# A perceiver layer on one core: keys and values as pairs of 64-row matmuls, and the heads' ends moved to ScalarE and GpSimd

## What is computed

```python
x = x + xattn(layernorm(x), ctx, ctx)      # 16 heads of 64, keys and values from ctx [8192, 512]
x = x + mamba_block(layernorm(x))          # selective scan, then a gated MLP
x = x + experts(layernorm(x))              # 16 experts, top 2, and a shared one

def xattn(Q, K, V):
    q = (Q @ Wq + bq) / sqrt(64)
    k, v = K @ Wk + bk, V @ Wv + bv        # [8192, 1024] each
    a = softmax(q @ k.T)                   # per head
    return (a @ v) @ Wo + bo
```

## Time and profile before

| | us |
|---|---|
| median of 3 runs | 2430.55 (2430.43 to 2432.51) |
| profiled execution | 2432.78 |
| its span | 2431.1 |
| PE busy | 2290.2 (94%) |
| DVE busy | 1974.1 (81%) |
| ACT busy | 1616.7 (67%) |
| POOL busy | 669.3 (28%) |
| key and value stage | about 41 to 864 |
| attention | about 864 to 1738 |

### The profile page before, as it was taken

The page is one execution under the profiler, slowest core; times in us unless marked ns, Lnnn a source line. Parts: engine busy times, 40 slices in busy tenths (PEclk is TensorE's granted clock), DMA queues, the critical chain, the costliest instruction groups (busy, mean ns, idle before and its releaser), DMA issues. The chain is left out here.

```text
span 2431.1 us, 45462 instructions
## 1 busy us (share of the span) xinstructions
PE 2290.2 (94%) x17215; PEld 1187.6 (49%) x17215; DVE 1974.1 (81%) x1972; ACT 1616.7 (67%) x1974; POOL 669.3 (28%) x464
## 2 busy tenths in 40 slices
PE   7999999999999978999999999999877788989998
PEld 3333333333333346666666666666432234444554
DVE  5777777777777788999999999999679992367996
ACT  5555565555655367989999889998474442237994
POOL 1455555555555430000000000000049970020001
PEclk9999999999999989999999999999989999999999
DMA  7244555445553397333333333331240014249994
GB/s 259 88 157 156 181 166 173 156 156 179 166 174 104 114 231 201 104 100 102 107 103 101 108 101 102 102 107 61 107 174 0 0 51 157 105 155 346 407 406 166
DMA packets 168861, 360.50 MB, mean 148 GB/s; under 512 B 13337, under 2 KB 84121, under 8 KB 165081
## 3 DMA queue, kind: packets, MB, share of 16 engines
q1 hardware_dynamic: 167266, 355.27, 45.4%
q0 software_dynamic: 1280, 4.20, 0.5%
q10 hardware_dynamic: 248, 0.15, 0.0%
HBM read 252.54 MB, written 107.04 MB: 148 GB/s over the span
## 5 line engine op out<-in xcount | busy, mean ns | idle before, releaser
L473 DVE TENSOR_REDUCE kv_mx<-kv_s 128x1024 f32 (+1 forms) x512 | 595.5, 1218 | 222.6 <-PE kv_s L509 222.6
L767 DVE TENSOR_TENSOR at_pl<-at_pf,at_ph 128x1024 f16<-128x1024 f32 x512 | 621.8, 1224 | 28.1 <-ACT at_ph L716 14.1
L722 ACT ACTIVATE at_pf<-at_st 128x1024 f32<-128x1024 f32 x512 | 521.7, 1020 | 91.2 <-PE at_st L869 90.3
L842 PE MATMUL at_acc<-at_vs,at_ph 128*128 128x130 f16 x4096 | 427.5, 220 | 17.0 <-DVE at_av L773 13.9
L844 PE MATMUL at_acc<-at_vs,at_pl 128*128 128x65 f16 x4096 | 413.1, 192 | 0.0
L842 PEld LDWEIGHTS at_acc<-at_vs,at_ph 128*128 128x128 f16 x4096 | 367.4, 97 | 86.2 <-DVE at_av L773 19.8
L868 PE MATMUL at_st<-keep_big,at_k_cur 128*128 (+1 forms) x1024 | 389.4, 380 | 13.9 <-DMA keep_big<-q_dram 7.6
L844 PEld LDWEIGHTS at_acc<-at_vs,at_pl 128*128 128x128 f16 x4096 | 362.2, 98 | 57.8 <-issue 0.3
L869 PE MATMUL at_st<-keep_big,at_k_one 128*128 (+1 forms) x1024 | 389.6, 380 | 0.0
L716 ACT ACTIVATE at_ph<-at_pf 128x1024 f16<-128x1024 f32 x256 | 268.4, 1048 | 0.0
L1083 POOL MEMSET mamba_zero<- 128x2 f32 x1 | 0.1, 99 | 855.0 <-POOLq L60 855.0
(11 more groups left out here) (348 smaller groups left out, 3595.9 us busy)
## 6 DMA issues: line engine op xcount, KB each, us to landing
keep_big<-gate_up SPq DMA_DIRECT2D x17, 2048.0 KB, 13.4
at_vs<-vd SPq DMA_DIRECT2D x64, 520.0 KB, 3.6
at_k_cur<-kd SPq DMA_DIRECT2D x126, 256.0 KB, 3.8
vd<-kv_vs SPq DMA_DIRECT2D x15, 2080.0 KB, 8.2
kv_tf<-wpack SPq DMA_DIRECT2D x21, 1024.0 KB, 6.3
keep_big<-down SPq DMA_DIRECT2D x17, 1024.0 KB, 13.6
first_cf<-ctxT SPq DMA_DIRECT2D x16, 1024.0 KB, 12.5
ex_yg<-gate_up SPq DMA_DIRECT2D x8, 2048.0 KB, 13.7
```

The costliest lines, as they stand in the source:

```text
L473: nc.vector.reduce_max(mx[:, bass.ds(g * (NH * TT) + 2 * (m - TT), 2)], s1[:, m % 3, :, :], AX.X).then_inc(s1_max, 1)
L722: nc.scalar.activation(pf[:, s % FULL, :, :], st[:, s % HP % NST, :, :], ACT.Exp, scale=SCORE).then_inc(pf_ready, 1)
L767: nc.vector.tensor_tensor(pl[:, s % RING, :, :], pf[:, s % FULL, :, :], ph[:, s % RING, :, :], ALU.subtract).then_inc(pl_ready, 1)
L842: nc.tensor.matmul(own_acc[t], ph[:, s % RING, e, tok], vs[:, 2 * s + e, :], start=first, stop=False, skip_group_check=True)
```

## The change

In the key and value stage each 128-row matmul of a unit becomes two 64-row matmuls, a top on rows 0 to 63 and a bottom on rows 64 to 127, which accumulate in the same bank one after the other: the top of matmul `k` of a unit is queued next to the bottom of matmul `k - 3` (`DELAY`) of the unit before, which is in another bank, so `kp` and `vp` get two banks each and `s1` keeps two buffers instead of three. A unit's bottoms begin once its tops are done (`top_done`). Score tiles are no longer in bursts: two of them stand in each unit, after matmuls 1 and 7, seven tiles behind the count of two per unit (`BEHIND`); seven are left after chunk 15. Two more passes of `units` finish the last bottoms.

In the attention, at a head's end ACT makes the two copies of `acc`, behind its exponential of step `HP + 3` (`COPY_AT`), POOL adds and multiplies, and DVE takes only the reciprocal, behind step `HP + 5`. At the last head ACT copies after its last step, DVE does the rest.

```diff
-        kp, vp = m.ps("kp", [P, CK]), m.ps("vp", [P, CK])
-        s1 = m.ps("s1", [P, 3, 2, CK])
+        kp, vp = m.ps("kp", [P, 2, CK]), m.ps("vp", [P, 2, CK])
+        s1 = m.ps("s1", [P, 2, 2, CK])
...
+        SCORES = PAIRS * TT
+        BEHIND = 7
+        SLOTS_OF_SCORES = (1, 7)
+        UNITS = 2 * PAIRS
+        DELAY = 3
...
+            def scores(g, par, n):
...
+                pe.wait_ge(kh_ready, PAIRS * g + n // TT + 1)
+                pe.wait_ge(s1_max, g * SCORES + n + 1)
+                for e in range(2):
+                    rows = slice(e * DH, (e + 1) * DH)
+                    nc.tensor.matmul(s1[:, n % 2, e, :], keep.qh[rows, j, t * P:(t + 1) * P],
+                                     keys[rows, j, :], start=True, stop=True,
+                                     tile_position=(rows.start, 0)).then_inc(s1_ready, 1)
...
+            def top(unit, k):
+
+                bank, pairs, _ = unit
+                a, b = pairs[k]
+                first = nc.tensor.matmul(bank, a[0:DH, :], b[0:DH, :], start=(k == 0), stop=False,
+                                         skip_group_check=True, tile_position=(0, 0))
+                if k == 11:
+                    first.then_inc(top_done, 1)
+
+            def bottom(unit, k, tops):
+
+
+                bank, pairs, done = unit
+                a, b = pairs[k]
+                if k == 0:
+                    pe.wait_ge(top_done, tops)
+                last = nc.tensor.matmul(bank, a[DH:P, :], b[DH:P, :], start=False, stop=(k == 11),
+                                        skip_group_check=True, tile_position=(DH, 0))
+                if k == 11:
+                    last.then_inc(done, 1)
+
+            def units(g, par, b, now, before, before2):
+
+
+                for k in range(12):
+                    if now:
+                        top(now, k)
+                    if k < DELAY and before2:
+                        bottom(before2, 12 + k - DELAY, None)
+                    elif k >= DELAY and before:
+                        bottom(before, k - DELAY, UNITS * g + b)
+                    if k in SLOTS_OF_SCORES:
+                        scores(g, par, 2 * b + SLOTS_OF_SCORES.index(k) - BEHIND)
...
+            units(NCK, 0, 0, None, unit(1, UNITS - 1), unit(1, UNITS - 2))
+            units(NCK, 0, 1, None, None, unit(1, UNITS - 1))
+            for n in range(4 - BEHIND, 0):
+                scores(NCK, 0, n)
...
+            with pool.Fori(0, NH - 1) as h:
+                pool.wait_ge(acc_read, h * 2 + 4)
+                nc.gpsimd.tensor_tensor(osum[:, :, :], av[:, :, 0:DH], av[:, :, ONE + 2:VW], ALU.add).then_inc(sum_ready, 1)
+                pool.wait_ge(sum_ready, h + 1)
+                pool.wait_ge(rc_ready, h + 1)
+                nc.gpsimd.tensor_tensor(o[:, :, bass.ds(h * DH, DH)], osum[:, :, :],
+                                        rc[:, :].unsqueeze(2).to_broadcast([P, TT, DH]), ALU.mult).then_inc(o_ready, 1)
...
-        END_AT, CUT = 1, 20
+        END_AT, COPY_AT, CUT = 5, 3, 20
...
+            def copied(h):
+                act.wait_ge(pv_done, h * HP + HP + RING)
+                act.wait_ge(o_ready, h + 1)
+                for b in range(2):
+                    nc.scalar.activation(av[:, 2 * b:2 * b + 2, :],
+                                         acc[:, b, 0:2 * VW].rearrange("p (t c) -> p t c", c=VW),
+                                         ACT.Copy).then_inc(acc_read, 1)
...
+                if s == HP + COPY_AT:
+                    copied(h)
...
             turns(act, pair, CUT)
+            copied(NH - 1)
...
             def end(h):
-                dve.wait_ge(pv_done, h * HP + HP + RING)
-                for b in range(2):
-                    nc.vector.tensor_copy(av[:, 2 * b:2 * b + 2, :], acc[:, b, 0:2 * VW].rearrange("p (t c) -> p t c", c=VW)
-                                          ).then_inc(acc_read, 1)
                 dve.wait_ge(acc_read, h * 2 + 4)
+                nc.vector.reciprocal(rc[:, :], av[:, :, ONE]).then_inc(rc_ready, 1)
...
-                pe.wait_ge(o_ready, 2 * j + 2)
+                pe.wait_ge(o_ready, 2 * j + 3)
```

More of the change, by code:

```diff
@@ L445, in _ @@
             act.wait_ge(mt_ready, 1)
-            nc.scalar.activation(mrow[:, :], kp[0:NH * TT, 0:P], ACT.Copy).then_inc(mrow_ready, 1)
+            nc.scalar.activation(mrow[:, :], kp[0:NH * TT, 0, 0:P], ACT.Copy).then_inc(mrow_ready, 1)
             act.wait_ge(mrow_ready, 1)
@@ L498, in _ @@
         def _(pe):
[L499 to L511, removed]
@@ L513, in scores_free @@
-            def scores_free(g, tiles):
-                if isinstance(g, int) and g == 0 and tiles[-1] < TT:
-                    return
-                pe.wait_ge(kh_ready, PAIRS * g + tiles[-1] // TT)
-                pe.wait_ge(s1_max, g * (PAIRS * TT) + tiles[0] - TT + 2)
-            def chunk(g, par, uses, i, tiles):
[L521 to L530, removed]
+            def scores(g, par, n):
+                if isinstance(g, int) and g == 0 and n < 0:
+                    return
+                j, t = n // TT % PAIRS, n % TT
+                keys = ksh[par if n >= 0 else 1 - par]
+                pe.wait_ge(kh_ready, PAIRS * g + n // TT + 1)
[5 more added lines that the diff above has]
+                                     tile_position=(rows.start, 0)).then_inc(s1_ready, 1)
@@ new lines, in key_unit, with value_unit @@
+            def key_unit(par, n):
+                cols = slice(n * P, (n + 1) * P)
+                return kp[:, n % 2, :], [p for c in range(DC) for p in three(
+                    keep.wkh[:, c, cols], keep.wkl[:, c, cols], ch[par][:, c, :], cl[par][:, c, :])], k_ready
+            def value_unit(par, n):
+                tok, cols = slice(n // 2 * P, (n // 2 + 1) * P), slice(n % 2 * 512, (n % 2 + 1) * 512)
+                return vp[:, n % 2, :], [p for c in range(DC) for p in three(
+                    ch[par][:, c, tok], cl[par][:, c, tok], keep.wvh[:, c, cols], keep.wvl[:, c, cols])], v_ready
@@ L532, in chunk, with unit @@
+            def unit(par, b):
+                return value_unit(par, b // 2) if b % 2 else key_unit(par, b // 2)
+            def chunk(g, par, uses, i, tiles):
                 pe.wait_ge(ch_ready, g + 1)
                 pe.wait_ge(cl_ready, g + 1)
[L534 to L543, removed]
+                for b in range(UNITS):
+                    if b % 2:
+                        pe.wait_ge(vf_ready, VT * g + b // 2 + 1)
+                    else:
+                        pe.wait_ge(kf_ready, PAIRS * g + b // 2 + 1)
+                    prior = [unit(par, b - n) if b >= n else None if isinstance(g, int) and g == 0
+                             else unit(1 - par, UNITS + b - n) for n in (1, 2)]
+                    units(g, par, b, unit(par, b), *prior)
@@ L789, in _ @@
             low(1)
-            end(NH - 1)
+            last_end()
             for j in range(2, PAIRS - 1):
```

55 lines of the change are left out of this document (25 added, 30 removed).

## The result

The changed kernel took 2396.73 us (median of four runs, 2396.10 to 2400.49) beside 2431.20 for the kernel before on the same chip: a ratio of 0.986, 95% interval 0.9845 to 0.9875, or 34.5 us faster. Forecast were 47.2. Its profiled execution has a span of 2394.7 us, 36.4 less than before. First the page: PE's busy time, and the queues' lines.

What follows compares the result with a forecast made beforehand. PE's queue was taken to bound both stages, with DVE and ACT close behind in the attention. Gains of 34.3 + 15.3 - 2.4 = 47.2 us gave 2383.5 us for the median, range 2377 to 2408.

Steps and rivals of the forecast that it cites:

- rival (b): Key and value stage: PE's longer loop body no longer stays loaded, 8 to 25 us, say 12, giving 2396; chance 0.12.
- What bounds it: Both stages: PE's queue leads; in the attention DVE (49.93) and ACT (45.95 of 51.00 us) stand right behind.
- Part 1, burst costs: Key and value stage: each score burst's 0.213 us beyond its work goes, 16 chunks x 11, 37.5 us.
- The pair at 0.2158, not 0.227: Key and value stage: a pair of halves takes 0.2158 us; 0.227 throughout would cost 40 us.
- (c): Key and value stage: accumulating pairs don't keep 0.2158 us; at 0.25 they cost 122 us, giving 2505; chance 0.10.
- (d): Key and value stage: pairs partly overlap or `kh_ready` is late, gaining half of 34, 2400; chance 0.08.
- Weight loads hidden, waits free: Key and value stage: doubled weight loads hide behind running matmuls, and PE's added waits cost nothing.
- The loop stays loaded: Key and value stage: PE's larger loop body of two chunks is not fetched again at its returns, no cost.
- The stage's end, +3.2: End of the key and value stage: last bottoms run with nothing beside them, net 3.2 us longer.
- Heads' ends: Attention: with ACT copying, an end loses 0.22 us instead of 1.24, 15 x 1.02 = 15.3 us gained.
- Rival (a): Attention: ACT or DVE falls behind after the copy, nothing gained at heads' ends, 2399; chance 0.12.
- The last head: Attention's end: ACT's copies come before its first `oh`, delaying PE's projection by 2.4 us, bounds 1.5 to 4.

Runs made afterwards that it cites:

- unrolled: The changed kernel with PE's loop over chunks written out, 16 chunks one after the other, other engines keeping their loops: 2388.96 us, ratio 0.9814.
- switch_each: The changed kernel's schedule of single score pairs, but with whole 128-row products in place of tops and bottoms: 2494.89 us.
- fill18: The changed kernel with 18 idle matmuls of 512 columns where PE waits for the first context: 2404.11 us, ratio 0.9884.
- best: The changed kernel with PE's chunk loop written out, 18 idle matmuls before the stage, and the last head's two copies back on DVE: 2379.52 us, ratio 0.9779.
- seven_moved: The changed kernel with one of three products left out of value units and 90 idle matmuls of 32 columns ahead of PE's loop: 2317.26 us.
- before_body4: The kernel before with PE's loop body doubled to four chunks, 2140 instructions and two returns: 2445.35 us beside 2435.73.

## Why the prediction was right, and where it was off

The sign and the stated range held. The median lies 13 us above the predicted time and outside the forecast's own bounds (2378 to 2391): it falls in the wider range because rival (b), given 0.12, came true, and the missing gain is where (b) had put it, at 2396. The account that the forecast itself rested on was right in every other part that it names.

- **What bounds it.** Right: both stages follow PE's queue.
- **Part 1, burst costs.** Right, 37.5 us. In `unrolled` the stage from first matmul to transpose is 786.7 us against 819.1 before, 32.5 less; the forecast was 34.3, and the slow start takes 1.7 of it. `switch_each` shows the 0.213.
- **The pair at 0.2158, not 0.227.** Right, for all 3584. Rivals (c) and (d) are refuted: chunk intervals of 48.35, and between 100 and 742 us no row of a wait for `kh_ready`, `s1_max` or `top_done`. The 0.227 is a first step after a change only.
- **Weight loads hidden, waits free.** Right.
- **The loop stays loaded.** This is the step that failed, and it had been given 0.12. Rival (b) named the mechanism, seven or eight packets against a limit that no row showed, and 12 us; measured 10.3 over six returns. I had counted seven, one too many: seven turns have six returns. What argued against it, "a body of five is not fetched again", was true and no evidence on eight. The Trainium skill (Advanced Engine Details and Errata, ISA Cache) gives 128 KB on TensorE in lines of 16 KB. By that size alone a body touching eight lines stays, and the traces disagree: it is fetched again, nine packets a return, seven stay.
- **The start of the stage.** Not foreseen: 1.7 us more at the 1.2 GHz level. The stage's first halves find PE's clock down after its wait. `fill18` and `best` hold it at 1.00 there.
- **The stage's end, +3.2.** Right within 0.2 us. The last top starts at 827.63 and the last bottom at 831.54, 3.91 us later and not 3.67: 18 steps, one more than counted. The chain behind it, to the next stage's first instruction, is 10.5 us against 10.7. It agrees with the balance of `unrolled` above (34.3 - 1.7 = 32.6 against 32.5).
- **Heads' ends.** 1.07 us each, forecast 1.02; a copy took 0.384, estimated 0.38. POOL's two operations took 0.81 and 1.34 us and not 0.6 each, and as forecast it cost nothing. Rival (a) is refuted. The first two heads, which wait for DMA, were shorter by 3.7 and 0.5, more than the 1.07 each that the change gives them; those differ from run to run (the first takes 53.8 us here and 57.2 in `unrolled`), so some 2 us of the profiled gain are luck.
- **The last head.** 2.3 us lost, forecast 2.4. Moved back, it was regained in full.
- **The rest.** Later stages took 2.5 us longer in the profiled execution. The experts' stage lies between 275.5 and 279.4 us in the kernels' profiles, whatever the edit, so 2 us of it I do not put down to the change.

From 47.2: less 10.3 for the returns, 1.7 for the start, 2.5 for later stages, plus 3.7 in the attention (0.7 from the longer gain per head, the rest mainly from the first heads) is 36.4, which is the difference of the spans.

## What to carry to other kernels

Where 64-row matmuls stand among whole ones, count the changes between the two, not the matmuls; if the whole ones can be cut in halves that run in pairs, all changes go. Before an edit makes a loop's body larger, count its instructions in packets of 256, from where the loop begins, and look at the instruction queue's packets after it: with eight or more touched, each return cost 1.5 to 6.6 us, and writing the loop out cost nothing. The numbers of 256 and of eight are what these runs bear out for TensorE. Where TensorE waits before a stage, its clock may be down when the stage begins; matmuls that fill the wait can hold it up, but they are instructions too and may move a loop.

## What the runs showed of the hardware

- TensorE's loop is not loaded again with seven packets touched (46 in all), and is with eight (101, 102) or nine (70 with two returns, 108 with six): 9 and 10 packets a return, one more than touched. The counts of touched packets are mine, from the built programs. This fits eight places for packets with one always being filled ahead, an inference that no run tests further.
- The price of a return was 1.5 to 2.0 us (changed kernel), 2.2 to 4.0 (`fill18`), 3.8 to 6.6 (`seven_moved`) and 3.7 to 6.5 (`before_body4`). It had up to three parts: the jump's gap; a second one 3.0 to 4.7 us behind it (in the one looked at, the next packet had not come); and slow matmuls where the clock fell to the 1.2 GHz level, 1.6 to 3.3 us a return. The two dearest returns of `fill18` (4.0 and 3.8) are the two with the fallen clock. What sets the spread of the jump's gap itself (1.5 to 2.0 in the changed kernel) is open, and so is why the clock falls behind some returns of a kernel and not behind others.
- Two half matmuls that accumulate in different banks, one on the upper and one on the lower rows, kept 0.2158 us a pair over all chunks, with two weight loads each. The Trainium skill's efficiency of 3.07 for four row tiles (TensorE: Matmul & The Clock Gate, Part 3) says nothing of two: no loss was seen.
